# Gates and mask preparation moved later, keys and values moved one slot later over two pairs of banks, and unread products before the scores

## The chip, the cores and the metric

The kernel runs on one core of one Trainium2 chip. The metric is the device time of one execution in microseconds (us), lower is better. Three runs of the kernel before were timed, and one more execution was profiled. The engines are named PE (TensorE), DVE (VectorE), ACT (ScalarE), POOL (GpSimd) and SP (SyncE, which here only issues loads and stores).

## The reference, cut to what matters

One decoder layer in three parts, for 8 sequences of 128 tokens with 256 features:

```python
x = x + gated_delta_attention(layernorm(x))       # 16 heads, DK = 128, VE = 256
x = x + cross_attention(layernorm(x), ctx, mask)  # 16 heads of 8, softmax with a mask
x = x + ffn(layernorm(x))                         # shared expert + top 2 of 8 experts
```

The first part, for every head:

```python
q, k = l2norm(silu(conv4(xn @ Wq))), l2norm(silu(conv4(xn @ Wk)))
v = silu(conv4(xn @ Wv))
alpha, beta = sigmoid(xn @ Wa), sigmoid(xn @ Wb)   # the "gates"
state = state * alpha_t                            # for every t
state = state + beta_t * k_t (v_t - state k_t)
out_t = state q_t ;  result = out @ Wo
```

The second part treats features as rows: queries, keys and values are products of a 128x128 matrix with 128 rows of 256 columns, one per sequence, plus bias; scores are `mask * q.k / sqrt(8) - (1 - mask) * 1e6`, then softmax and the product with the values.

## The kernel before, in words

Every engine has its own program, written out by hand; semaphores (`wait_ge`, `then_inc`) tie them together. So the order of the work is the order in which the functions are called on each engine.

**Start.** SP loads x and the constants, then the weights of the first heads. DVE takes the moments of x (`moments`, L898, L901), ACT turns them into a scale (`norm_act`, L649, L651), DVE normalises (L907), PE turns the result (L1264), ACT copies it out as 32-bit and 16-bit values (L660, L662), DVE takes the low half (L919, `xtl`). PE makes the gate products with Wa and Wb (L1269), DVE copies them (L921), ACT takes Abs, Exp and Ln (L665 to L669), DVE forms `gl` (L928), PE sums over time (L1272), DVE copies and subtracts (`gcum` L930, `gcol` L933). DVE also prepares the mask rows (`mask5`, L924, L936) and the bias rows (`bias5`, L925, L938, L940) for the second part. POOL issues eight loads for the second part (L445), and then splits the weights of a head into 16-bit high and low halves (`split`, L455 to L461).

**The loop of steps.** 32 steps: 16 heads, each for two groups of 4 sequences. `slots` calls `slot(k)` for k = -3 to 33 on every engine, and one slot holds different stages of neighbouring steps: `a` (step k+2) is projected (`proj_`, L1294: 6 products of 512 columns for each of 4 tiles), biased by ACT (L697) and convolved by DVE (`tap`, L1004, 3 for each tile); its squares are split (POOL `sql`, L477). `b0` (step k+1) has its norms (L1322, L1323), logs (ACT L723), exponents (L1339, L1344) and Gram products (L1354, L1364), and DVE multiplies these with the decay (`lm`, L1016, L1027). `b` (step k) inverts a triangular matrix by levels: POOL cuts out the levels (`ct`, L491), PE multiplies (L1374, L1382, L1389, L1392), ACT copies (L679, L684), DVE subtracts (L958 to L987). `z` (L1310) multiplies values with Wo. `c` (step k-1) does the last levels, a residual (L1440 to L1442) and `y` (L1452, L1453, L1463), and `d` (step k-2) the output products (`outp`, L1474), which DVE adds to x (L1034, L1041). Slot 30 has no projection any more, slot 31 no exponents, slot 32 and 33 only `c` and `d`.

Projections and z use the banks `ubank` (PSUM banks 0 and 1), exponents and Gram products `ebank` (2 and 3).

**Keys and values of the second part.** In slots 30 and 31 (`STEPS - 2`, `STEPS - 1`), `kv(n)` handles one sequence bb = 0 to 7 for n = 0 to 3: first the value product of the sequence before (`v_proj`, L1480), then four key products (L1503, each with its bias, L1504) into `ubank`; ACT copies both halves (`k_split`, L768), DVE stacks them (`kv_stack`, `kst`, L1078) and adds the value bias (`v_add`, L1065). POOL masks the context for this at the end of slot 29 (L548).

```python
if m == 1:
    need(pe, v_ready, 2 * bb)
for g2 in range(2):
    o = ubank[hh][:, g2 * H:(g2 + 1) * H]
```

**Scores.** After the loop 64 units follow, four for each of 16 heads. For each unit PE makes `top_scores` (L1584: 4 products of 32 rows) into one of three pairs of banks, DVE reduces it to maxima (`maxima`, L1138); nine units later PE makes `energies` (L1605, 4 products of 32 rows), ACT takes the exponentials (L817), and PE multiplies with the values (`values`, L1619). `pair_free` waits until the pair of banks has been read. Per head there are also query products (`q_proj`, L1571, L1572), their copy (ACT L811) and stacking (DVE L1131), and the turning of the maxima (L1594). Then the feed-forward part follows, which the change doesn't touch.

Of the kernel before, what the change touches and what calls it, by code (L numbers as in the profile page):

```python
# [17 lines left out]
ALU = mybir.AluOpType  # L18
# [103 lines left out]
def build(nc, d, out):  # L122
    with ExitStack() as whole:
# [86 lines left out]
        zrow = zz[0:5].rearrange("p r j n -> p (r j n)")  # L210
# [73 lines left out]
        names = ("x_loaded", "consts_loaded", "xattn_loaded", "experts_loaded", "ffn_loaded", "stored")  # L284
        x_loaded, consts_loaded, xattn_loaded, experts_loaded, ffn_loaded, stored = [sem(n) for n in names]
# [37 lines left out]
        ebank = [bank[2], bank[3]]  # L323
        bt, bx, ctk, cx = [quad[:, n, :] for n in range(4)]
# [35 lines left out]
        def _(sp):  # L360
            for b in range(B):
                sp.dma_start(x1[:, b, :], x_in[:, b, :]).then_inc(x_loaded, 16)
# [63 lines left out]
        def _(pool):  # L426
# [15 lines left out]
            for dst, src in ((maskrow[:], d["mask_row"].partition_broadcast(P)),  # L442
                             (wks[:], d["xk"]), (wvt[:], d["xv"]), (stackcol[:], d["stackcol"]), (biasf, d["xbias"]),
                             (bvrow[:], d["bv_row"].partition_broadcast(P)), (maskcol[:], d["mask_col"]), (wqs[:], d["xq"])):
                g.dma_start(dst, src).then_inc(xattn_loaded, 16)  # L445

# [17 lines left out]
            pool.wait_ge(xn_done, B)  # L464
            split(0, 0, None)
            def slot(k):
# [187 lines left out]
        def _(act):  # L654
            s = nc.scalar
            norm_act(act, 0, slice(0, B))

            for b in range(B):
                act.wait_ge(xt_psum, b + 1)
                s.activation(xt[:, :, b * T:(b + 1) * T], bank[b % 2][:, 0:H].rearrange("p (c t) -> p c t", c=CH), ACT.Copy).then_inc(xt_full, 1)  # L660
# [3 lines left out]
            act.wait_ge(gate_step, 1)  # L664
            s.activation(ga[:], gz[:], ACT.Abs).then_inc(gate_act, 1)  # L665
            act.wait_ge(gate_act, 1)
            s.activation(ga[:], ga[:], ACT.Exp, scale=-1.0).then_inc(gate_act, 1)
            act.wait_ge(gate_act, 2)
            s.activation(ga[:], ga[:], ACT.Ln, bias=1.0).then_inc(gate_act, 1)  # L669

            def slot(k):
                f, a, b0, b, c, d = [k.at(n) for n in (3, 2, 1, 0, -1, -2)]

# [87 lines left out]
                def k_split(n):  # L761

                    if k.i is None and k.c in (STEPS - 2, STEPS - 1):
                        bb = (k.c - STEPS + 2) * 4 + n
                        for m in range(2):
                            act.wait_ge(k_psum, 2 * bb + m + 1)
                            need(act, k_stack, 2 * bb + m - 1)
                            s.activation(kh[:, 1 - m], ubank[1 - m], ACT.Copy).then_inc(k_high, 1)  # L768
# [19 lines left out]
                bias(1)  # L788
                k_split(1)
# [120 lines left out]
        def _(dve):  # L910
# [5 lines left out]
            for b in range(B):  # L916
# [3 lines left out]
            dve.wait_ge(gate_psum, 1)  # L920
            v.tensor_copy(gz[:], bank[2][:, 0:B * 2 * HK]).then_inc(gate_step, 1)  # L921
            dve.wait_ge(xattn_loaded, 16 * 8)
            dve.wait_ge(mask_cast, 1)
            v.tensor_copy(mask5[0:4], maskrow[0:4]).then_inc(mask_cast, 1)  # L924
            v.tensor_copy(biash, biasf).then_inc(bias_cast, 1)  # L925
            dve.wait_ge(gate_act, 3)
            dve.wait_ge(gate_step, 1)
            v.scalar_tensor_tensor(out=gl[:].rearrange("p b n -> p (b n)"), in0=gz[:], scalar=0.0, in1=ga[:], op0=ALU.min, op1=ALU.subtract).then_inc(gate_step, 1)  # L928
            dve.wait_ge(cum_psum, 1)
            v.tensor_copy(gcum[:].rearrange("p h b -> p b h"), bank[3][:, 0:B * HK].rearrange("p (b h) -> p b h", b=B)).then_inc(gates_done, 1)  # L930
            dve.wait_ge(gates_done, 1)
            dve.wait_ge(gate_step, 2)
            v.tensor_tensor(gcol[:].rearrange("p h b -> p b h"), gl[:, :, HK:], gcum[:].rearrange("p h b -> p b h"), ALU.subtract).then_inc(gates_done, 1)  # L933
            dve.wait_ge(mask_cast, 2)
            m5 = mask5[0:4].rearrange("p b n -> p (b n)")
            v.scalar_tensor_tensor(out=m5, in0=m5, scalar=stackcol[0:4, 3:4], in1=maskrow[0:4].rearrange("p b n -> p (b n)"), op0=ALU.mult, op1=ALU.add).then_inc(mask_ready, 1)  # L936
            dve.wait_ge(bias_cast, 1)
            v.tensor_copy(bias5[:], biash).then_inc(bias_cast, 1)  # L938
            dve.wait_ge(bias_cast, 2)
            v.scalar_tensor_tensor(out=bias5[0:4].rearrange("p k g n -> p (k g n)"), in0=biash[0:4].rearrange("p k g n -> p (k g n)"),  # L940
                                   scalar=stackcol[0:4, 2:3], in1=biasf[0:4].rearrange("p k g n -> p (k g n)"), op0=ALU.mult, op1=ALU.add).then_inc(bias_ready, 1)

            def slot(k):
# [877 lines left out]
```

## Time and profile before

| | |
|---|---|
| Timed runs | 937.96 (median), 933.4, 1081.68 us |
| Profiled execution, its own time | 934.79 us |
| Span, first to last instruction | 932.9 us |
| PE busy | 828.1 us (89%) |
| DVE busy | 719.7 us (77%) |
| ACT busy | 617.8 us (66%) |
| POOL busy | 540.2 us (58%) |
| Mean granted clock of PE | 0.94 |

The granted clock is a share of 2.4 GHz; PE has two levels, 1.2 GHz (0.5) and 2.4 GHz (1.0). Times in rows count from the first instruction. In rows of the timeline and of the chain the first number is the start, the second the duration in us; "x12" says how many instructions a row merges.

### The profile page before, as it was taken

To read this page: it belongs to the slowest core of one execution; us is meant where nothing else is said; L and a number is where in the kernel's file an instruction comes from. 1 tells how busy PE (TensorE), PEld (TensorE's weight loads), DVE (VectorE), ACT (ScalarE), POOL (GpSimd) and SP (SyncE) were. 2 spreads that over 40 slices of the span, in tenths; PEclk is the share of its full clock that TensorE was granted. 3 is DMA by queue.
4 is the path that set the end of the run, shared out by engine and by line. 5 is a ranking of instruction groups with operands and counts; after the bars stand their busy time and mean duration, and the time that the engine had idled before them with its cause. 6 is when DMAs were issued, how large, how long until landed. Compare 5 with 4: busy or idle time off the path is not lost.

```text
span 932.9 us, 21903 instructions
## 1 busy us (share of the span) xinstructions
PE 828.1 (89%) x7371; PEld 531.5 (57%) x7408; DVE 719.7 (77%) x1227; ACT 617.8 (66%) x1022; POOL 540.2 (58%) x689
## 2 busy tenths in 40 slices
PE   3578999999999999999999999998867898889997
PEld 2245776677667766777677767765543333323353
DVE  7768888888888888887888788884556756674746
ACT  3377887788778877887888778873230565567522
POOL 6439769678696796886966968574302232322300
PEclk9989999999999999999999999999985777778999
DMA  6202010010110100101101000000001500000000
GB/s 194 57 1 80 1 35 27 11 35 0 34 34 0 34 19 15 34 0 34 34 0 34 10 23 11 2 2 1 1 1 27 94 15 18 16 14 25 10 23 24
DMA packets 34416, 23.98 MB, mean 26 GB/s; under 512 B 5062, under 2 KB 33414, under 8 KB 34235
## 3 DMA queue, kind: packets, MB, share of 16 engines
q1 hardware_dynamic: 31643, 19.00, 7.2%
q0 software_dynamic: 2720, 4.29, 2.2%
q8 instruction: 32, 0.52, 0.2%
q14 instruction: 21, 0.17, 0.1%
HBM read 22.68 MB, written 1.05 MB: 25 GB/s over the span
## 4 chain that ended last, share of the span: by engine, by line
PE 66%; DVE 17%; issue 9%; ACT 5%; POOL 2%; DVEq 1%; DMA 0%; SPq 0%; ACTq 0%; POOLq 0%
PE psum L1294 13%; PE psum L1310 11%; PE psum L1474 6%; DVE y L1004 6%; PE psum L1619 3%; PE psum L1571 3%; PE psum L1364 3%; PE psum L1354 3%; DVE mx L1138 3%; DVE ux L984 3%; PE psum L1382 2%; PE psum L1503 2%; PE psum L1389 1%; PE psum L1392 1%; PE psum L1708 1%
## 5 line engine op out<-in xcount | busy, mean ns | idle before, releaser
L1004 DVE SCALAR_TENSOR_TENSOR y<-psum,cwh,y 128x508 f32<-128x508 f32 (+2 forms) x384 | 281.5, 740 | 18.4 <-ACT y L697 12.4
L491 POOL TENSOR_TENSOR ct<-lm,levels 128x256 f16<-128x256 f32 x224 | 152.0, 701 | 18.4 <-DVE lm L1027 18.4
L477 POOL TENSOR_TENSOR sql<-sq,sqh 128x1024 f16<-128x1024 f32 x32 | 68.4, 2137 | 126.3 <-ACT sq L744 126.3
L697 ACT ACTIVATE y<-psum,cwh 128x512 f32<-128x512 f32 x128 | 99.4, 777 | 50.8 <-PE psum L1294 50.8
L1310 PE MATMUL psum<-wo,vt 128*128 128x256 f32 x512 | 126.0, 389 | 1.2 <-DVE y L1004 1.0
L1310 PEld LDWEIGHTS psum<-wo,vt 128*128 128x128 f32 x512 | 92.3, 190 | 11.9 <-DVE y L1004 2.0
L817 ACT ACTIVATE et<-psum 128x1024 f32<-128x1024 f32 x64 | 65.2, 1022 | 43.3 <-PE psum L1605 43.3
L1138 DVE TENSOR_REDUCE mx<-psum 128x4 f32<-128x1024 f32 x64 | 77.2, 1219 | 21.4 <-PE psum L1584 21.3
L1294 PE MATMUL psum<-xth,whi 128*128 128x512 f16 x256 | 78.0, 387 | 8.7 <-DVE y L1004 5.4
L984 DVE TENSOR_TENSOR ux<-ux,psum 128x512 f16<-128x512 f16 x64 | 43.9, 686 | 53.8 <-PE psum L1392 52.7
L1294 PE MATMUL psum<-xth,wlo 128*128 128x512 f16 x256 | 78.0, 387 | 0.0
L1294 PE MATMUL psum<-xtl,whi 128*128 128x512 f16 x256 | 77.9, 387 | 0.0
L509 POOL TENSOR_TENSOR lml<-lm,lmh 128x1024 f16<-128x1024 f32 x32 | 68.3, 2135 | 0.0
L972 DVE TENSOR_TENSOR ux<-ux,psum 128x512 f16<-128x512 f16 x96 | 65.1, 678 | 1.1 <-PE psum L1392 0.8
L1389 PEld LDWEIGHTS psum<-t1z,ux 128*128 128x128 f16 x768 | 46.9, 98 | 32.4 <-ACT t1z L679 2.5
L1382 PE MATMUL psum<-ux,ct 128*128 128x64 f16 x768 | 54.7, 194 | 11.3 <-DVE ux L984 7.3
L1474 PE MATMUL psum<-zz,pt 128*128 128x256 f32 x256 | 62.4, 388 | 0.7 <-ACT pt L717 0.7
L499 POOL TENSOR_TENSOR lmh<-lm,zero 128x1024 f16<-128x1024 f32 x32 | 60.5, 1891 | 0.0
L1389 PE MATMUL psum<-t1z,ux 128*128 128x64 f16 x768 | 54.3, 194 | 3.4 <-ACT t1z L684 1.9
L595 POOL TENSOR_SCALAR mxs<-mx 128x16 f32<-128x16 f32 x16 | 4.0, 253 | 88.2 <-DVE mx L1138 88.2
L1474 PEld LDWEIGHTS psum<-zz,pt 128*128 128x128 f32 x256 | 49.5, 194 | 7.9 <-ACT pt L717 1.0
L1382 PEld LDWEIGHTS psum<-ux,ct 128*128 128x128 f16 x768 | 36.7, 97 | 30.0 <-DVE ux L984 12.7
(215 smaller groups left out, 2016.6 us busy)
## 6 DMA issues: line engine op xcount, KB each, us to landing
wraw<-in_L_attn_Wv SPq DMA_DIRECT2D x32, 128.0 KB, 2.7
wo<-in_L_attn_Wo SPq DMA_DIRECT2D x16, 256.0 KB, 2.8
wraw<-in_L_attn_Wk SPq DMA_DIRECT2D x16, 128.0 KB, 2.5
wraw<-in_L_attn_Wq SPq DMA_DIRECT2D x16, 128.0 KB, 2.7
moved<-avs SPq DMA_DIRECT2D x128, 16.0 KB, 1.8
x<-in_x SPq DMA_DIRECT2D x8, 128.0 KB, 4.1
maskrow<-in_mask_row POOLq DMA_DIRECT2D x1, 1024.0 KB, 4.5
xt<-in_ctx SPq DMA_DIRECT2D x1, 1024.0 KB, 6.1
```

Source lines behind the costliest of these rows:

```text
L477: g.tensor_tensor(lo, f, hi, ALU.subtract).then_inc(sq_split, 1)
L491: g.tensor_tensor(dst, src, pick.unsqueeze(1).to_broadcast([P, NB, T // (2 * m), m]), ALU.mult).then_inc(masked[l], 1)
L509: g.tensor_tensor(lo, f, hi, ALU.subtract).then_inc(lm_low, 1)
L697: s.activation(y[:, n], ubank[n % 2].rearrange("p (j t) -> p j t", j=NB), ACT.Identity, scale=cwh[:, (a.c // 2) % 2, n, TAPS - 1:TAPS], bi ...
L984: v.tensor_tensor(changed(r, m), changed(r, m), cx.rearrange("p (a q u) -> p a q u", a=2, u=m), ALU.subtract).then_inc(uxc_sb, 1)
L1004: v.scalar_tensor_tensor(out=y[:, n, :, sh:], in0=u[:, :, 0:T - sh], scalar=cwh[:, (a.c // 2) % 2, n, TAPS - 1 - sh:TAPS - sh], in1=y[:, n ...
L1138: v.tensor_reduce(mx[:, h % 2, g2, 2 * rp:2 * rp + 2].rearrange("p r a -> p (r a)"), pair_of("max", n).rearrange("p r (a s) -> p (r a) s", ...
L1294: mm = t.matmul(ubank[n % 2], w_[:, hr, n, ch, :], x_[:, ch, cols], start=(m == 0), stop=(m == len(ops) - 1))
L1310: mm = t.matmul(ubank[n][:, j * H:(j + 1) * H], vt[:, r, vc, (2 * n + j) * T:(2 * n + j + 1) * T], wo[:, hr, vc, :], start=(vc == 0), stop ...
L1382: mm = t.matmul(half(dst[:, j * 64:(j + 1) * 64], m), ct[:, st.c % 2, level, j], first_half(turned(st.c % 2, 1, j), m), start=True, stop=True)
L1389: mm = t.matmul(half(dst[:, 256 + j * 64:256 + (j + 1) * 64], m), turned(st.c % 2, 0, j), first_half(t1z[:, level - 1, j * T:(j + 1) * T], ...
L1474: mm = t.matmul((ctk, cx)[hf][:, jj * H:(jj + 1) * H], pt[:, j], zz[:, d.c % 2, j], start=True, stop=True)
```

## The change

1. Start: a semaphore for each x load, so that the moments of a sequence wait only for its own load. ACT loads at once the table set that holds both Exp and Ln. The turned x goes through other banks (4 and 5). POOL's eight loads for the second part stand behind the first split, which no longer waits for the normalised x. PE's first projections wait for 4 and then 8 low halves only.
2. Gates: products, activations and sums move from ahead of the loop into slot -2, between its projections and taps. The bias rows are prepared at the end of slot -1 (`prepare_bias`), the mask rows at the end of slot 0 (`prepare_mask`), both on DVE.
3. Keys and values: slots 31 and 32 instead of 30 and 31; sequences alternate between `ubank` and `ebank` (`kbank`), and a sequence's key products stand ahead of the value product of the one before.
4. Scores: `warm` puts products of 128 rows and 256 columns, 16-bit, that nobody reads, into the pair of banks ahead of the real ones: 3 before the maxima of the first 8 units, 4 before the exponents of the first 8, 1 before the exponents of the others.

```diff
-            for dst, src in ((maskrow[:], d["mask_row"].partition_broadcast(P)),
...
-                g.dma_start(dst, src).then_inc(xattn_loaded, 16)
...
             pool.wait_ge(conv_scaled, 3)
-            pool.wait_ge(xn_done, B)
             split(0, 0, None)
+            for dst, src in ((maskrow[:], d["mask_row"].partition_broadcast(P)),
...
         def _(act):
             s = nc.scalar
+            s.preload_act_table_set("natural_log_exp_and_others")
             norm_act(act, 0, slice(0, B))
...
-                    dve.wait_ge(x_loaded, 16 * B)
+                    dve.wait_ge(x_loaded[b], 16)
...
+                def prepare_bias():
+
+                    if k.i is None and k.c == -1:
+                        dve.wait_ge(xattn_loaded, 16 * 8)
+                        v.tensor_copy(biash, biasf).then_inc(bias_cast, 1)
...
+                def prepare_mask():
+
+                    if k.i is None and k.c == 0:
+                        dve.wait_ge(xattn_loaded, 16 * 8)
...
                 def kv_stack(n):
 
-                    if not (k.i is None and k.c in (STEPS - 2, STEPS - 1)):
-                        return
-                    bb = (k.c - STEPS + 2) * 4 + n
-                    if n > 0:
-                        v_add(bb - 1)
+                    if not (k.i is None and k.c in (STEPS - 1, STEPS)):
+                        return
+                    bb = (k.c - STEPS + 1) * 4 + n
...
                     pe.wait_ge(w_split, a.head + 1)
+                    if k.i is None and k.c in (-2, -1):
+                        pe.wait_ge(xt_low, (k.c + 3) * NB)
...
+                def gate_products():
+
+                    if k.i is None and k.c == -2:
+                        for b in range(B):
+                            pe.wait_ge(xt_full, b + 1)
...
                     for m in range(2):
                         hh = 1 - m
+                        need(pe, k_stack, 2 * (bb - 1))
                         if m == 1:
-                            need(pe, v_ready, 2 * bb)
+                            need(pe, v_ready, 2 * (bb - 1))
                         for g2 in range(2):
-                            o = ubank[hh][:, g2 * H:(g2 + 1) * H]
+                            o = kbank[bb % 2][hh][:, g2 * H:(g2 + 1) * H]
...
+                    if n > 0:
+                        v_proj(bb - 1)
...
+            def warm(out, b, gq, count):
+
+                for w in range(count):
+                    t.matmul(out[:, w % 2, 0:H], ident16[:], kst[:, b, gq, :], start=True, stop=True)
+
             def top_scores(n):
...
                 pair_free("max", n)
+                warm(pair_of("max", n), b, gq, 3 if n < 8 else 0)
...
                 pair_free("exp", n)
+                warm(pair_of("exp", n), b, gq, 4 if n < 8 else 1)
```

DVE's order before the first tap and in slot -2. Names are tiles, out<-in; L numbers are lines of the program shown. Before:

```order
L919 TENSOR_TENSOR xtl<-xt,xth 128x2x128 [waits xt_high] x8
L921 COPY gz<-psum 128x256 [waits gate_psum]
L924 CAST mask5<-maskrow 4x2048 [waits mask_cast,xattn_loaded]
L925 CAST zz<-zz 5x1024
L928 SCALAR_TENSOR_TENSOR gl<-gz,ga 128x256 [waits gate_step,gate_act]
L930 COPY gcum<-psum 128x8x16 [waits cum_psum]
L933 TENSOR_TENSOR gcol<-gl,gcum 128x8x16 [waits gate_step,gates_done]
L936 SCALAR_TENSOR_TENSOR mask5<-mask5,stackcol,maskrow 4x2048 [waits mask_cast]
L938 COPY bias5<-zz 5x1024 [waits bias_cast]
L940 SCALAR_TENSOR_TENSOR bias5<-zz,stackcol 4x1024 [waits bias_cast]
L1004 SCALAR_TENSOR_TENSOR y<-psum,cwh,y 128x4x127 [waits biased0]
```

And after the change, from the low halves on, with the end of slot -1 as its last rows (L1025 is `tap`, L1048 `lmul_later`, which was L1027):

```order
L924 TENSOR_TENSOR xtl<-xt,xth 128x2x128 [waits xt_high] x8
L1025 SCALAR_TENSOR_TENSOR y<-psum,cwh,y 128x4x127 [waits biased0]
...
L932 COPY gz<-psum 128x256 [waits gate_psum]
L1025 SCALAR_TENSOR_TENSOR y<-psum,cwh,y 128x4x127 [waits biased2]
...
L939 SCALAR_TENSOR_TENSOR gl<-gz,ga 128x256 [waits gate_step,gate_act]
L941 COPY gcum<-psum 128x8x16 [waits cum_psum]
L944 TENSOR_TENSOR gcol<-gl,gcum 128x8x16 [waits gate_step,gates_done]
...
L950 CAST vv<-vv 5x1024 [waits xattn_loaded]
L952 COPY bias5<-vv 5x1024 [waits bias_cast]
L954 SCALAR_TENSOR_TENSOR bias5<-vv,stackcol 4x1024 [waits bias_cast]
L1048 TENSOR_TENSOR lm<-psum,decay 128x512 [waits decayed,kq_psum]
```

The taps moved ahead of the gates, and the bias rows now stand directly ahead of `lm`; the mask rows stand in the same way ahead of the `lm` of slot 1.

PE's order at a sequence of keys and values in the middle of slot 31. Before, the value product comes first and the second half of the keys waits for `v_ready`:

```order
L1480 MATMUL psum<-wvt,xt 128x128 [waits k_stack]
L1480 MATMUL psum<-wvt,xt 128x128
L1503 MATMUL psum<-xt,wks 128x256 [waits ctx_masked]
L1504 MATMUL psum<-mask5,bias5 128x256
L1503 MATMUL psum<-xt,wks 128x256
L1504 MATMUL psum<-mask5,bias5 128x256
L1503 MATMUL psum<-xt,wks 128x256 [waits v_ready]
L1504 MATMUL psum<-mask5,bias5 128x256
L1503 MATMUL psum<-xt,wks 128x256
L1504 MATMUL psum<-mask5,bias5 128x256
```

After (L1537 and L1538 are the key products, L1513 is `v_proj`):

```order
L1537 MATMUL psum<-xt,wks 128x256 [waits ctx_masked,lm_done]
L1538 MATMUL psum<-mask5,bias5 128x256
L1537 MATMUL psum<-xt,wks 128x256
L1538 MATMUL psum<-mask5,bias5 128x256
L1537 MATMUL psum<-xt,wks 128x256
L1538 MATMUL psum<-mask5,bias5 128x256
L1537 MATMUL psum<-xt,wks 128x256
L1538 MATMUL psum<-mask5,bias5 128x256
L1513 MATMUL psum<-wvt,xt 128x128 [waits k_stack]
L1513 MATMUL psum<-wvt,xt 128x128
```

The value product moved behind the keys of the next sequence, and these no longer wait for `v_ready` here.

PE's order at the first unit of scores, after the change (L1617 is `warm`, L1628 `top_scores`, which was L1584; L1609 and L1610 are the query products):

```order
L1609 MATMUL psum<-xm,wqs 128x256
L1610 MATMUL psum<-mask5,bias5 128x256
L1617 MATMUL psum<-kst,ident16 128x256 [waits q_stack]
L1617 MATMUL psum<-kst,ident16 128x256 x2
L1628 MATMUL psum<-kst,qst 128x256 x4
```

Before, the four products of the unit follow the query products directly. The wait moved from them to the first unread product.

## Rows read from the trace of the kernel before

**Rows 1.** The page, part 4: the chain that ended last, by engine.

```profile
PE 66%; DVE 17%; issue 9%; ACT 5%; POOL 2%; DVEq 1%; DMA 0%; SPq 0%; ACTq 0%; POOLq 0%
```

**Rows 2.** Timeline of the start, 12 to 38 us.

```profile
12.35 1.28 ACT L651 ACT_TABLE_LOAD   x1
12.68 0.60 POOL L445 DMA_DIRECT2D maskrow<-in_mask_row  x1
...
17.43 1.91 POOL L455 TENSOR_TENSOR wraw<-wraw,c 128x1024 f32<-128x1024 f32 x1
...
19.73 6.88 PE L1269 MATMUL psum<-wab,xt 128*128 128x32 f32 x32
...
22.01 2.31 POOL L461 TENSOR_TENSOR wlo<-wraw,whi 128x1024 f16<-128x1024 f32 x1
...
27.10 0.42 ACT L665 ACTIVATE ga<-gz 128x256 f32<-128x256 f32 x1 [6.08 <-DVE gz L921]
...
32.74 2.33 DVE L936 SCALAR_TENSOR_TENSOR mask<-mask,stackcol,maskrow 4x2048 f16<-4x2048 f16 x1
32.83 2.31 POOL L459 COPY cwh<-cb 128x4 f32<-128x4 f32 x1
...
32.93 1.01 PE L1294 MATMUL psum<-xth,whi 128*128 128x512 f16 x2 [1.25 <-issue]
...
35.45 3.03 DVE L940 SCALAR_TENSOR_TENSOR bias<-zz,stackcol 4x1024 f16<-4x1024 f16 x1
```

**Rows 3.** The chain in order of time, slots -2 and -1.

```profile
42.33 0.61 ACT y L697
...
48.11 2.13 POOL sql L477
...
50.94 5.11 PE psum L1294 x12
```

**Rows 4.** Timeline at the ends of slots -1 and 0.

```profile
64.93 0.68 DVE L1027 TENSOR_TENSOR lm<-psum,decay 128x512 f32<-128x512 f32 x1
...
66.74 2.75 POOL L491 TENSOR_TENSOR ct<-lm,levels 128x256 f16<-128x256 f32 x4
...
84.81 2.76 POOL L491 TENSOR_TENSOR ct<-lm,levels 128x256 f16<-128x256 f32 x4
```

**Rows 5.** Chain, slots 30 to 33; the last two rows: timeline, ordinary slot.

```profile
637.66 0.96 PE psum L1480 x4
...
674.03 0.71 PE psum L1480 x4
...
677.95 0.61 ACT kh L768
...
679.38 0.71 PE psum L1480 x4
...
698.48 3.79 PE psum L1474 x8
...
703.94 1.19 PE psum L1571 x2
...
614.12 0.39 PE L1344 MATMUL psum<-rows,select 128*128 128x128 bf16 x4
...
622.92 1.97 PE L1310 MATMUL psum<-wo,vt 128*128 128x256 f32 x8
```

**Rows 6.** Windows: length, busy us per engine (instructions), PEclk, DMA share, GB/s; last, line L1584.

```profile
657.80:687.00 29.20, 25.20 (x182) 16.08 (x179) 15.83 (x28) 8.90 (x18) 8.75 (x9) 1.00 0.01 1
...
712.80:724.40 11.60, 8.57 (x46) 3.50 (x48) 11.33 (x12) 0.60 (x1) 2.19 (x7) 0.50 0.01 1
724.40:841.50 117.10, 102.63 (x965) 36.04 (x961) 79.38 (x94) 67.88 (x85) 31.53 (x90) 0.76 0.17 32
...
762.00:769.70 7.70, 6.33 (x74) 2.48 (x74) 5.77 (x8) 5.05 (x7) 2.15 (x8) 1.00 0.03 8
...
L1584 PEld LDWEIGHTS psum<-kst,qst x256: 90/94/147, 711.1 to 841.9; 32*128 32x128 f16 x128
```

More of the change, by code:

```diff
@@ L927, in _ @@
[L927 to L941, printed above, removed]
@@ L943, in slot, with gate_raw, gate_sums @@
             def slot(k):
                 f, a, b0, b, c, d = [k.at(n) for n in (3, 2, 1, 0, -1, -2)]
+                def gate_raw():
+                    if k.i is None and k.c == -2:
+                        dve.wait_ge(gate_psum, 1)
+                        v.tensor_copy(gz[:], bank[2][:, 0:B * 2 * HK]).then_inc(gate_step, 1)
+                def gate_sums():
+                    if k.i is None and k.c == -2:
+                        dve.wait_ge(gate_act, 3)
+                        dve.wait_ge(gate_step, 1)
+                        v.scalar_tensor_tensor(out=gl[:].rearrange("p b n -> p (b n)"), in0=gz[:], scalar=0.0, in1=ga[:], op0=ALU.min, op1=ALU.subtract).then_inc(gate_step, 1)
+                        dve.wait_ge(cum_psum, 1)
+                        v.tensor_copy(gcum[:].rearrange("p h b -> p b h"), bank[3][:, 0:B * HK].rearrange("p (b h) -> p b h", b=B)).then_inc(gates_done, 1)
+                        dve.wait_ge(gates_done, 1)
+                        dve.wait_ge(gate_step, 2)
+                        v.tensor_tensor(gcol[:].rearrange("p h b -> p b h"), gl[:, :, HK:], gcum[:].rearrange("p h b -> p b h"), ALU.subtract).then_inc(gates_done, 1)
@@ new lines, in prepare_mask @@
+                def prepare_mask():
+                    if k.i is None and k.c == 0:
+                        dve.wait_ge(xattn_loaded, 16 * 8)
+                        dve.wait_ge(mask_cast, 1)
+                        v.tensor_copy(mask5[0:4], maskrow[0:4]).then_inc(mask_cast, 1)
+                        dve.wait_ge(mask_cast, 2)
+                        m5 = mask5[0:4].rearrange("p b n -> p (b n)")
+                        v.scalar_tensor_tensor(out=m5, in0=m5, scalar=stackcol[0:4, 3:4], in1=maskrow[0:4].rearrange("p b n -> p (b n)"), op0=ALU.mult, op1=ALU.add).then_inc(mask_ready, 1)
@@ L1263, in _ @@
                 for c in range(CH):
[L1264 removed]
+                    mm = t.transpose(quad[:, b % 2, c * P:(c + 1) * P], xn[:, b, c * P:(c + 1) * P], ident[:])
                 mm.then_inc(xt_psum, 1)
[L1266 to L1274 removed]
             def slot(k):
@@ L1295, in proj_, with gate_totals @@
                     mm.then_inc(proj[n], 1)
+                def gate_products():
+                    if k.i is None and k.c == -2:
+                        for b in range(B):
+                            pe.wait_ge(xt_full, b + 1)
+                            for c in range(CH):
+                                mm = t.matmul(bank[2][:, b * 2 * HK:(b + 1) * 2 * HK], xt[:, c, b * T:(b + 1) * T], wab[:, c, :], start=(c == 0), stop=(c == CH - 1))
+                        mm.then_inc(gate_psum, 1)
+                def gate_totals():
+                    if k.i is None and k.c == -2:
+                        pe.wait_ge(gate_step, 2)
+                        t.matmul(bank[3][:, 0:B * HK], tri[:], gl[:, :, 0:HK], start=True, stop=True).then_inc(cum_psum, 1)
                 def z(n):
@@ L1317, in norms @@
                     pe.wait_ge(sq_split, b0.count(1, 1))
+                    if k.i is None and k.c == -1:
+                        pe.wait_ge(gates_done, 2)
                     need(pe, lm_done, b0.count(2, 0))
@@ L1479, in v_proj @@
                     for st in range(2):
-                        mm = t.matmul(ubank[0][:, st * P:(st + 1) * P], ctxs[:, bb, st * P:(st + 1) * P], wvt[:], start=True, stop=True)
+                        mm = t.matmul(kbank[bb % 2][0][:, st * P:(st + 1) * P], ctxs[:, bb, st * P:(st + 1) * P], wvt[:], start=True, stop=True)
                     mm.then_inc(v_psum, 1)
                 def kv(n):
-                    if not (k.i is None and k.c in (STEPS - 2, STEPS - 1)):
+                    if not (k.i is None and k.c in (STEPS - 1, STEPS)):
                         return
-                    bb = (k.c - STEPS + 2) * 4 + n
+                    bb = (k.c - STEPS + 1) * 4 + n
                     if bb == 0:
```

89 lines of the change are left out of this document (44 added, 45 removed).

## The prediction

> **What bounds the kernel now.** I read the page's chain first [rows 1]: it runs over TensorE (PE) for 66% of the span and over VectorE (DVE) for 17%, so PE's order and clock decide, and another engine only where PE waits for it. Then, stage by stage, the places that the diff touches.
>
> At the start [rows 2] the first projection stands at 32.93 us. Ahead of it: POOL (GpSimd) issues eight loads from 12.68, splits the first weights from 17.43 to 24.32 (22.01 + 2.31), PE makes the gate products until 26.61, and ACT and DVE turn them into sums. The chain goes on over the third bias at 42.33, the square's low half on POOL at 48.11, and 12 projection products at 5.11 us, which is 427 ns for 512 columns, the 1.2 GHz level [rows 3].
>
> At the loop's end [rows 5] a batch's keys and values repeat every 5.35 us (674.03 to 679.38): 3.92 us of products, then ACT's copy, DVE's stacking and again PE, over one pair of banks. The last output products take 3.79 us at 698.48, half speed.
>
> In the scores [rows 6] the granted clock is 0.76 on average over 117 us, while PE is busy for 102.6 of them. A head (four units) takes 7.7 us where the clock is 1.00; the mean head of the 13 in this stretch takes 9.0. Before that, from 712.8 to 724.4, DVE is busy for 11.33 of 11.6 us: there PE's clock costs nothing.
>
> **The change part by part**, against the profiled execution's own 934.8 us (1.9 around its span of 932.9; the median shown is 3.2 higher, the lowest run 1.4 lower).
>
> *Start, first half.* POOL no longer issues eight loads or waits for x before the first split, so the split can start a little behind 12.68, say 12.9, if the raw weights are there, and ends 6.89 later at 19.8. Statistics per batch and a table load fewer (1.28) bring x forward too; they are hidden, since the projection now waits for the split. First projection: 20.1, 12.8 earlier. Its twelve products at 1.2 GHz take 5.11, the gate products 6.88 behind them, DVE's copy and ACT's three steps (0.42 each, no load between, as both functions are in one set now) about 1.85: 33.9 [rows 2, 3]. There the third bias can run, which ran at 42.33; 0.1 for hand-over, and I take 34.1: -8.2. The taps of the first two tiles lie under the gate products. The gate sums stand between tap 3 of tile 2 and tile 3 (about 2 us, and the last tile's taps then end near 42, beside the low half of the squares, which ends at 42.2 instead of 50.2). Shift here: -8.0. Bounds: -9.5 if the gate products run at the full clock, -6 if weights land 2 us late.
>
> *Start, given back.* The casts and stackings that stood in the shadow of the gates now stand on DVE ahead of the product lm of L1027, at the end of slots -1 and 0; behind lm wait POOL's ct, then PE's first level and all that follows. The bias part in slot -1: POOL's sql starts just ahead of it and ends with the start of ct at 66.74; behind it come two copies (estimate 0.8, a third of the mask's 2.33), the stacking (half of 2.33, 1.2; the rest of its 3.03 at 35.45 was a wait), then lm 0.6: ct 2.6 later [rows 2, 4]. In slot 0 the mask's stacking 2.33 and its cast, taken as half of that, make 3.5; lm and with it ct (84.81) is late by this, less what slack there is, plus a POOL pass caught between: 3.4. Together +6.0. Bounds: +2.6 if nothing collides and most of it passes beside POOL's sql, +8 if POOL is caught twice. Net start -2.0 (-6 to +1).
>
> What a collision does is in rows 2: POOL's copy of 128x4 at 32.83 lasts 2.31 us, as long as DVE's stacking at 32.74; the stacking at 35.45 lasts 3.03 for half the elements of the one that took 2.33. The Trainium skill (SBUF — State Buffer, "Who interferes with whom") says that DVE, with two SBUF inputs or in a two-port mode, and GpSimd take a shared port pair for a whole instruction and the second blocks fully. By that rule the +6.0 stands and +2.6 would be out of reach, as POOL's wlo and sql passes stand there; the trace agrees with it.
>
> *Keys and values a slot later.* Slot 30 loses its four batches. Until 637.66 nothing changes (POOL masks the context there). From there to the start of z at 657.8 [rows 6] it took 20.1; what is left is what an ordinary slot has from its exponents at 614.12 to z at 622.92, 8.8 us, less two projections, each half of what six products take in rows 3, 1.3 [rows 3, 5]: 6.2; I take 6.7, as one more copy stands in series there. Gain 13.4. Slot 31 keeps four batches, now over two pairs: three stalls of 5.35 - 3.92 go, 4.3, but 2.6 of other products stood in them: -1.7. Slot 32 (687.0 to 698.48, 11.5, waits for the most part) takes four batches of 3.92, 15.7, and a last wait of 1.4; 5.5 of it fills that slot's waits: +11.6. The output products then run behind a busy PE at 2.4 GHz: -1.9. Sum -5.4 (-3 to -8).
>
> *Entry to the scores.* The eight query products from 703.94 (1.19 for two) with copy and stacking between them would take 5.4 instead of 8.1 at full clock. I take -2.0 (0 to -2.7), as PE waits twice for 1.5 us there.
>
> *Unread products.* 24 stand before the first 8 maxima, 32 before the first 8 exponents, 56 before the others; a 256-column product takes half of what 512 columns take [rows 3], 0.21 at 1.2 GHz and 0.107 at 2.4. The first 24 lie under DVE's maxima: 8.57 + 24 x 0.21 = 13.7 at half clock would be 2.1 over the 11.6, at full clock there is room: 0. Then 13 heads. With p the share at 1.2 GHz, a head takes 7.65 + 2.8 p: 0.76 is p = 0.48 and gives 9.0, as measured. Four products add 0.43 at full clock and 0.85 at half, of which DVE's work covers some: 0.3 and 0.6 net. What p becomes, no row says. In the slot of 657.8 to 687.0 PE is busy for 86% with whole-array products and has 1.00; in the scores 88% with 32-row products gives 0.76. So whole-array products keep the clock where strips don't, and I take p = 0.2, a bit nearer to the loop: 13 x (7.65 + 0.56 + 0.35) = 111.3 instead of 117.1, -5.8, and +2.0 for the extra 24 of the first exponents: -3.8. Bounds: p = 0, -11.6; p as before, +8.
>
> Each group of four 32-row products loads its weights in 94 ns [rows 6], now beside products in flight. If a whole-array product ahead of the group uncovers that load, the 72 groups with one pay 72 x 0.094 = 6.8 us on PE; I leave it out of the sum and make it a rival.
>
> The Trainium skill (TensorE: Matmul & The Clock Gate, "Part 3: Packing small matmuls") states such a rule: a weight load overlaps products in flight only where their row groups differ, and a whole-array product shares all of them. No row quoted here shows whether it holds at this place.
>
> Sum: -2.0 - 5.4 - 2.0 - 3.8 = -13.2, 921.6; I say **922**.
>
> **The rivals.**
> *Clock held at 2.4 GHz through all scores.* For it: fast stretches of whole heads exist already (762.0 to 769.7). Against it: one product per unit is little. Scores -11.6, entry -2.7, start and loop end -7.4: 913.
> *The clock falls and rises as before.* The products then cost +8, the entry gives nothing: 934.8 - 7.4 + 8 = 935.
> *Slower.* The unread products stand between the bank's release and the real product, and at 1.2 GHz each is twice as dear; if the clock is at 1.2 for more of the scores than now, PE is the bound and they are all on its path. Place: the scores after the first maxima. Price at p = 0.6: 13 x (7.65 + 1.68 + 0.65) = 129.7, +12.6, and 5.5 for the first groups: 934.8 - 7.4 + 18 = 945. It decides from p of about 0.46 on. Against it: whole-array products are what the loop has, with 1.00.
> *Loads uncovered.* As worked out above, 6.8 us more on PE in the scores, 922 + 6.8 = 929. For it: the strips' loads have cover now and a whole-array product takes all rows. Against it: PE isn't on the path all the time in a head at full clock (6.33 of 7.7 busy).
> *The start isn't shorter.* If weights or DVE and POOL collisions eat all 8 us and the loop's end gives 3: 934.8 - 3 - 2 - 3.8 = 926.
>
> **How the numbers follow.** Forecast 0.38, clock held 0.25, as before 0.14, loads uncovered 0.10, start not shorter 0.07, slower 0.06. A measurement of this kernel can tell about 2% from no change: under 919.2 is faster, over 956.7 slower (against 937.96). Faster: 0.85 of the clock-held case and a quarter of the forecast, 0.31. Slower: a third of its case, 0.02. The range reaches from under the clock-held case to just over the as-before one: 911 to 936. It leaves out the slower case and some of the ends.
>
> **What would show it.** First projection near 20 us; POOL's first sql near 40; ct of slot 0 about 5.5 and of slot 1 about 2 us earlier than 66.7 and 84.8; z of the last step near 642; last output products at full clock, ending near 695; first maximum near 703.6. In the scores: mean granted clock of 0.9 and heads of 8.4 to 8.6 us. Wrong if the clock there stays under 0.8, if heads at full clock take over 8.1 us (the products cost more than counted), or if the first lm (L1027 before) doesn't come near 60.

## The result

| | median, us | runs | ratio to before, 95% interval |
|---|---|---|---|
| before | 936.2 | 933.4, 934.47, 937.96, 1081.68 | |
| changed | 993.7 | 990.57, 990.74, 996.69, 996.89 | 1.0619, 1.0571 to 1.0667 |

The changed kernel is 6.2% slower; I had said 922 us, 911 to 936. Its profiled execution took 990.57 us with a span of 988.8, against 934.79 and 932.9: 55.9 us more. The run of 1081.68 us is a slow one and isn't in the ratio.

The page of the changed kernel: PE's busy tenths and its clock in 40 slices (24.7 us each), the chain by engine (it answers to [rows 1]; the chain could only be followed back to 612.8 us, so its shares cover 38% of the span), and two groups of instructions with their busy time, mean ns and the idle time ahead of them.

```profile
PE   3678999999999999999999999798899999999897
...
PEclk9798999999999999999999999896755555557999
...
PE 32%; DVE 2%; issue 2%; ACT 1%; POOL 1%; DVEq 0%; POOLq 0%; ACTq 0%
...
L822 ACT ACTIVATE et<-psum 128x1024 f32<-128x1024 f32 x64 | 65.5, 1023 | 88.4 <-PE psum L1650 87.9
L1164 DVE TENSOR_REDUCE mx<-psum 128x4 f32<-128x1024 f32 x64 | 78.2, 1223 | 52.1 <-PE psum L1628 50.2
```

The same two groups on the page of before:

```profile
L817 ACT ACTIVATE et<-psum 128x1024 f32<-128x1024 f32 x64 | 65.2, 1022 | 43.3 <-PE psum L1605 43.3
L1138 DVE TENSOR_REDUCE mx<-psum 128x4 f32<-128x1024 f32 x64 | 77.2, 1219 | 21.4 <-PE psum L1584 21.3
```

The reader sees the loss in one look: seven slices in a row with PE at 9 and the clock at 5, and ACT and DVE, whose own work hasn't grown, waiting 45 and 31 us longer for PE's scores. Stretch by stretch (windows of the changed kernel, columns as in [rows 6]):

```profile
641.10:701.90 60.80, 52.79 (x318) 32.07 (x314) 32.46 (x67) 18.15 (x34) 9.56 (x11) 0.86 0.00 1
672.50:689.50 17.00, 15.74 (x65) 8.59 (x64) 5.60 (x14) 4.83 (x9) 0.00 (x0) 0.50 0.00 1
709.80:727.70 17.90, 17.63 (x83) 6.54 (x84) 13.17 (x14) 1.24 (x3) 2.18 (x7) 0.50 0.00 1
727.70:896.00 168.30, 168.30 (x1038) 50.80 (x1036) 81.97 (x92) 69.93 (x84) 31.57 (x90) 0.50 0.12 23
```

The fourth row answers to the third of [rows 6]: 168.3 us instead of 117.1, PE busy for all of it, the clock at 0.50 throughout instead of 0.76. The third answers to its second: the first maxima took 17.9 us instead of 11.6, and now PE is busy for 17.63 of them and DVE waits. The account: 2.0 us were gained up to the first query product (701.95 against 703.94), and 57.9 lost behind it (988.8 - 701.9 = 286.9 against 932.9 - 703.9 = 229.0).

Why a head costs so much stands in a timeline of one of its units at 1.2 GHz (L1628: the maxima's strips, 4 products of 32 rows; L1617: the unread product; L1650: the exponents' strips; L1664: values), with the starts of the query products one head apart:

```profile
786.17 1.22 PE L1609 MATMUL psum<-xm,wqs 128*128 128x256 f32 x2
...
794.06 0.61 PE L1628 MATMUL psum<-kst,qst 32*128 32x256 f16 x4
794.60 0.39 PE L1617 MATMUL psum<-kst,ident 128*128 128x256 f16 x1
794.93 0.61 PE L1650 MATMUL psum<-qst,kst 32*128 32x256 f16 x4
795.47 1.08 PE L1664 MATMUL psum<-et,vz 128*32 128x256 f32 x8
...
798.89 1.22 PE L1609 MATMUL psum<-xm,wqs 128*128 128x256 f32 x2
```

and in the kernel before, the last two units of a head in which the clock was at 1.2 GHz too (L1584, L1605, L1619 are the same products):

```profile
747.04 1.22 PE L1571 MATMUL psum<-xm,wqs 128*128 128x256 f32 x2
...
753.53 0.61 PE L1584 MATMUL psum<-kst,qst 32*128 32x256 f16 x4
754.19 0.61 PE L1605 MATMUL psum<-qst,kst 32*128 32x256 f16 x4
754.73 1.08 PE L1619 MATMUL psum<-et,vz 128*32 128x256 f32 x8
755.75 0.39 PE L1584 MATMUL psum<-kst,qst 32*128 32x256 f16 x2
755.76 0.40 PE L1605 MATMUL psum<-qst,kst 32*128 32x256 f16 x2
755.94 0.42 PE L1584 MATMUL psum<-kst,qst 32*128 32x256 f16 x2
755.95 0.42 PE L1605 MATMUL psum<-qst,kst 32*128 32x256 f16 x2
756.30 1.08 PE L1619 MATMUL psum<-et,vz 128*32 128x256 f32 x8
...
757.31 1.22 PE L1571 MATMUL psum<-xm,wqs 128*128 128x256 f32 x2
```

Before, the two sets of strips ran interleaved in the last unit: a strip of each started at the same moment, as one set uses two of the array's row groups and the other set (nine units behind, an odd number) the other two. All eight took 756.30 - 755.75 = 0.55 us. With a product of all rows between them they run one set after the other: 0.54 + 0.33 + 0.54 = 1.41. So the unread product cost 0.86 us where I had counted 0.21: 0.33 of its own, from its start to that of the next strip, and 0.53 of lost company. Not every unit had that much to lose. In the one behind the turning of the maxima (753.53) the exponents' strips wait for DVE's step on the turned maxima (L1126, 753.96), the sets ran one after the other before too, in 1.20 us, and the price was 0.21. The two units behind the query products took 0.74 and 0.75 and now 1.60 and 1.41. Over the four units that is 2.6 us, 0.65 on average. A head went from 10.27 (757.31 - 747.04) to 12.72 (798.89 - 786.17) at the same clock. The Trainium skill (TensorE: Matmul & The Clock Gate, "Part 3: Packing small matmuls") states the other half of the rule that I had cited: products in different row groups run at the same time in one array. The trace of before agrees (755.75 and 755.76), and I had not looked at what stood next to the place of the new product.

Two theories for the rest, and a third for the clock. *Between strips*: the products' place makes PE the bound at 1.2 GHz, and from there the clock doesn't come back. *Own time*: any further product would do it. *Entry*: the moved keys and values send PE into the scores with a low clock, and it stays there.

### The profile page after: what moved, and what is told of

It reads as the page before. It is cut to its first block and busy times, and to the rows that moved or that the text cites. A ratio compares the mean times of both kernels' runs of the same rounds, so it can differ in the third digit from the quotient of the medians.

```text
span 988.8 us, 22137 instructions
## 1 busy us (share of the span) xinstructions
PE 904.0 (91%) x7483; PEld 549.1 (56%) x7520; DVE 725.2 (73%) x1227; ACT 617.4 (62%) x1020; POOL 537.4 (54%) x689
## 5 line engine op out<-in xcount | busy, mean ns | idle before, releaser
L1025 DVE SCALAR_TENSOR_TENSOR y<-psum,cwh,y 128x508 f32<-128x508 f32 (+2 forms) x384 | 281.5, 740 | 21.7 <-ACT y L701 15.7
L1664 PE MATMUL psum<-et,vz 128*32 128x256 f32 x512 | 64.5, 596 | 0.0
```

Source lines behind the costliest of these rows:

```text
L1025: v.scalar_tensor_tensor(out=y[:, n, :, sh:], in0=u[:, :, 0:T - sh], scalar=cwh[:, (a.c // 2) % 2, n, TAPS - 1 - sh:TAPS - sh], in1=y[:, n ...
L1664: mm = t.matmul(avb[ps, gq // 2 * H:(gq // 2 + 1) * H], vz[:, b % 2, st, r, gq], et[:, gn % 4, r, st], start=(gq == 0 and st == 0), stop=( ...
```

## The experiments

All changes below are against the changed kernel unless "before" is said. The kernel before ran beside each set: 935.2, 933.7 and 933.5 us.

### Without the unread products, and each group of them alone

```diff
-                warm(pair_of("max", n), b, gq, 3 if n < 8 else 0)
+                warm(pair_of("max", n), b, gq, 0)
-                warm(pair_of("exp", n), b, gq, 4 if n < 8 else 1)
+                warm(pair_of("exp", n), b, gq, 0)
```

> The changed kernel without any unread product. Between strips: a whole-array product between the 32-row strips of two units ends their running side by side and costs about 0.6 us a unit at 1.2 GHz; without it heads go back to 9.0 us on average, the granted clock in the scores to about 0.76, and the time to 928 to 936 us (the scores began 3 us earlier than in the kernel before). Entry: the moved keys and values leave PE at 1.2 GHz and it stays there without the products too; the heads then take the 10.3 us that the slow heads of the kernel before took, and the time is about 960.

Measured: 931.5 us, ratio 0.995 (0.9921 to 0.9978). Windows of the first maxima, and from there to the last maximum:

```profile
714.70:727.10 12.40, 9.19 (x48) 3.64 (x48) 11.38 (x12) 1.13 (x3) 2.19 (x7) 0.50 0.01 2
727.10:841.20 114.10, 99.53 (x960) 35.28 (x960) 79.93 (x93) 67.47 (x85) 31.54 (x90) 0.79 0.17 33
```

The whole loss is gone, with the clock at 0.79 (0.76 in the kernel before). The entry theory fell here: with all the moves in place the stage doesn't stay low by itself.

The two groups apart: the first eight units only (3 and 4 products, none for the others), or the others only (0, and 1 at each exponent).

> The changed kernel with the unread products at the first eight maxima (3 each) and exponents (4 each) alone. Between strips: those 56 cost 6 to 12 us at most (exponents 4 x 0.21 to 0.33 us x 8 at 1.2 GHz), then heads go as in the kernel before: 932 to 944. Entry, or a clock that stays low once PE is filled: 965 or more, clock 0.5 through the scores.

Measured: 943.6 us, ratio 1.0097 (1.0063 to 1.013), 12 us over the run without any. The 56 products of the first groups don't hold the clock down afterwards, but they bring nothing back: they cost 0.21 us each, and in the profiled execution (948.33) the first rise of the clock comes at 748 instead of 735.

> The changed kernel with one unread product ahead of each exponent's strips from the ninth unit on, and none at the first eight. Between strips: close to the changed kernel, 975 to 992, clock 0.5 to 0.55 over the heads. Own time alone: 56 x 0.21 = 12 us over the run without any, 940 to 948, clock 0.7 or more.

Measured: 927.9, 942.77, 943.46 and 970.76 us. No ratio can be given; the clock took different courses in the four executions (its mean over the span was 0.952, 0.932, 0.932 and 0.891). Of the profiled one (943.46), two windows that follow each other:

```profile
739.00:810.70 71.70, 64.82 (x678) 24.41 (x674) 50.19 (x53) 45.03 (x55) 20.32 (x56) 1.00 0.14 27
810.70:855.10 44.40, 44.40 (x289) 13.36 (x290) 22.47 (x33) 20.60 (x26) 8.82 (x27) 0.50 0.05 13
```

My expected 975 to 992 was a miss: the product between the strips doesn't force the low clock. While the clock is at 1.00 it stays there for 71.7 us. But once it fell, at 810.7, after 2.70 us in which PE was busy for 1.94, it stayed down for 44.4 us with PE busy for all of them. In the kernel before, between the first rise at 735 and the last maximum, these are the longest stretches at either level:

```profile
745.50:759.10 13.60, 13.47 (x97) 4.30 (x97) 6.87 (x7) 6.93 (x9) 3.37 (x12) 0.50 0.08 21
786.40:806.80 20.40, 16.61 (x199) 6.36 (x191) 15.62 (x17) 13.24 (x17) 5.10 (x14) 1.00 0.07 19
```

So the product between the strips lengthens both: the high clock holds, and the low one does too.

### The same products, one place earlier

```diff
-                warm(pair_of("max", n), b, gq, 3 if n < 8 else 0)
+                warm(pair_of("max", n), b, gq, 0 if n < 8 else 1)
-                warm(pair_of("exp", n), b, gq, 4 if n < 8 else 1)
+                warm(pair_of("exp", n), b, gq, 0)
```

> The changed kernel with the same 56 unread products moved ahead of the maxima's strips from the ninth unit on, so that the maxima's and the exponents' strips stay next to each other. Between strips: they cost their own 0.21 to 0.33 us, strips still interleave, clock above 0.6, time 938 to 960, at least 20 us under the run with one per exponent. If any further product on PE does it, both runs take the same time.

Measured: 922.1 us, ratio 0.9863 (0.9805 to 0.9922); once more in the last set:

> The run with one unread product per maximum and all moves (922.1 before), once more for its interval: 920 to 925, ratio 0.985 to 0.99.

921.9 us, ratio 0.9889 (0.9872 to 0.9905): 1.1% under the kernel before, an interval clear of 1 but less than the 2% that I had set as a change, and 7% under the changed one. Windows of the first of the two runs (first maxima; up to the clock's rise; the rest), and its unit at 1.2 GHz, in which the strips of both sets start together again behind the unread product:

```profile
710.00:723.10 13.10, 10.07 (x50) 3.74 (x50) 11.66 (x13) 1.19 (x2) 2.19 (x7) 0.50 0.00 1
723.10:738.10 15.00, 14.32 (x101) 4.66 (x101) 10.06 (x11) 7.67 (x8) 4.72 (x11) 0.50 0.47 84
738.10:840.50 102.40, 92.65 (x1023) 36.68 (x1022) 75.02 (x93) 68.28 (x86) 29.77 (x85) 1.00 0.13 26
```

```profile
731.82 0.39 PE L1617 MATMUL psum<-kst,ident 128*128 128x256 f16 x1
732.15 0.39 PE L1628 MATMUL psum<-kst,qst 32*128 32x256 f16 x2
732.16 0.40 PE L1650 MATMUL psum<-qst,kst 32*128 32x256 f16 x2
732.33 0.42 PE L1628 MATMUL psum<-kst,qst 32*128 32x256 f16 x2
732.35 0.42 PE L1650 MATMUL psum<-qst,kst 32*128 32x256 f16 x2
732.70 1.08 PE L1664 MATMUL psum<-et,vz 128*32 128x256 f32 x8
```

The whole unit, from the unread product to the values, takes 732.70 - 731.82 = 0.88 us, against 1.41 in the changed kernel. And the clock holds at 1.00 for 102.4 us on end. What I had as a rival (the clock held through the scores) exists, with one product per unit, at this place.

The changed kernel with only its single product moved by that one place, the first groups left as they are:

```diff
-                warm(pair_of("max", n), b, gq, 3 if n < 8 else 0)
+                warm(pair_of("max", n), b, gq, 3 if n < 8 else 1)
-                warm(pair_of("exp", n), b, gq, 4 if n < 8 else 1)
+                warm(pair_of("exp", n), b, gq, 4 if n < 8 else 0)
```

> The changed kernel, with the single product from the ninth unit on put ahead of the maxima's strips instead of between them and the exponents' strips; the number of products stays. Between strips: the clock rises at 735 to 755 and holds, 925 to 940. If the products of the first eight groups alone send the stage into the low clock whatever follows: 975 or more.

Measured: 935.2 us, ratio 1.0012 (0.9978 to 1.0045). The number of unread products is the same as in the changed kernel, and it takes 58 us less. Its windows, while the clock was down and up, in an execution of 943.39 us; eight of its ten runs took 933 to 937, with a mean clock of 0.947 to 0.952 against 0.938 in this one, so the rise mostly came sooner than here:

```profile
709.60:764.20 54.60, 54.33 (x285) 18.90 (x283) 28.13 (x31) 12.62 (x15) 9.28 (x28) 0.50 0.29 52
764.20:859.80 95.60, 86.66 (x961) 34.37 (x957) 70.28 (x87) 64.49 (x82) 28.51 (x82) 1.00 0.07 18
```

The clock rises at 764 here, 26 us later than without the first groups (738), and then holds past the last maximum (853). This is the decisive pair: the place, not the number; the own-time theory falls with it. Read with the runs before it: without the first groups the clock mostly found its way up although the products stood between the strips, and with the first groups it found its way up as long as they didn't. The changed kernel has both, and there it stayed down to the end of the scores in the execution that was profiled; the mean clock of its four runs, 0.869 to 0.875, says the same of the others.

Next, the four at the first exponents are taken out too (3 at the first eight maxima, 1 at the others, none at an exponent).

> As the run before, and none at the first eight exponents either: 3 at the first eight maxima, 1 at every other maximum. Between strips: no unread product is left between strips, clock up by 740, 917 to 926, with that of one per maximum alone (922) in its middle; first maxima filled with products should bring the rise forward by 3 to 10 us, or take 2 us on PE. If the filling of the first maxima is what holds the clock down: 935 or more.

Measured: 926.5 us, ratio 0.9924 (0.9893 to 0.9955). So the 32 at the first exponents cost 8.7 us and the 24 at the first maxima 4.5 more (926.5 against 922); with them the clock rose at 741.3 instead of 738.1. I had expected it to come 3 to 10 us sooner: it doesn't.

### The products without the moves

```diff
--- before
+                warm(pair_of("max", n), b, gq, 3 if n < 8 else 0)
+                warm(pair_of("exp", n), b, gq, 4 if n < 8 else 1)
```

> The kernel before with the unread products of the changed kernel (3 at the first eight maxima, 4 at the first eight exponents, 1 at every other exponent) and nothing else of the change. Products alone: the clock stays at 0.5 through the heads, a head 12.7 us, 980 to 1000. If the moved keys and values or the moved gates are needed for it: clock as in the kernel before, 935 to 955.

Measured: 994.1, 996.0 and 996.2 us, and once 963.2. A window of the profiled one:

```profile
691.10:906.10 215.00, 207.76 (x1231) 67.86 (x1231) 106.37 (x135) 80.48 (x102) 42.16 (x115) 0.50 0.10 21
```

The unread products alone make the kernel before as slow as the changed one in three runs of four, and the fourth is still 3.2% over the kernel before. The moved gates, keys and values aren't needed for the loss. The one run at 963.2 has no trace; a clock that rose part of the way through would explain it, and its mean granted clock, 0.925 against 0.877 to 0.881 in the others, fits.

> The kernel before with one unread product ahead of the maxima's strips from the ninth unit on, and nothing else. The moved gates, keys and values brought 3.7 us in the run without products (931.5 against 935.2), so this should be 922 + 3.7 = 926, 922 to 930, with a clock of 1.00 for most of the heads. If the rise of the clock hangs on the moved parts: 932 or more.

(0 for the first eight, then 1 ahead of the maxima's strips, none at the exponents, and no other edit.) Measured: 925.6 us, ratio 0.9925 (0.9881 to 0.9969), the clock at 1.00 from 739.1 on. The gain doesn't hang on the moves either.

### The moves by themselves

The start alone (before, with the gates, loads, bias and mask as in the changed kernel):

> The kernel before with the start of the changed kernel (gates behind the first projection, loads behind the first split, bias and mask prepared in slots -1 and 0) and nothing else. The floors of the last step came 3.2 us earlier in the changed kernel (624.8 against 628.0) and 1.9 in the run without unread products, so 2 to 3 us less than before: 931 to 933. If what is left of my forecast for both moves (9.4 us) came from the start: 926 to 928.

Measured: 934.6 us, ratio 1.0009 (0.9986 to 1.0031). In its trace z of the last step came 2.9 us earlier than before (654.9), but the low clock that begins at the end of the loop lasted 51.2 us (688.8 to 740.0) instead of 44.3 (690.8 to 735.1).

Keys and values alone (before, with `kv`, `v_proj`, `k_split` and `kv_stack` a slot later over both pairs):

> The kernel before with the keys and values a slot later over two pairs of banks and nothing else. My forecast was 5.4 us less, and 2.0 less at the entry of the scores. In the changed kernel the granted clock fell to 0.5 for 17 us over these batches, in the kernel before it stayed at 1.00 there: if that eats the gain, 933 to 937, with the first query product at 703 to 709 against 703.9; if the forecast holds, 926 to 929 and the first query product near 698.

Measured: 934.6 us, ratio 1.0017 (0.9996 to 1.0039). Two stretches of its slots 31 and 32:

```profile
656.20:666.50 10.30, 10.30 (x44) 5.93 (x43) 3.54 (x7) 2.17 (x4) 0.00 (x0) 0.51 0.01 2
680.10:697.20 17.10, 15.84 (x66) 8.47 (x67) 5.97 (x16) 5.50 (x10) 0.00 (x0) 0.51 0.00 1
```

In the kernel before, the granted clock was 1.00 over the batches but for 3.4 us around 638 (slot 31: first row of [rows 6]). Here 27 us of slots 31 and 32 ran at half speed; its first query product came at 710.4, 6.5 us later than before.

> The changed start, keys and values as before, one unread product ahead of the maxima's strips from the ninth unit on. If keys and values a slot later bring nothing: 922 to 924, level with the run that has them. If they are worth what I forecast: 927 or more.

Measured: 924.8 us, ratio 0.9909 (0.9877 to 0.9941), 2.8 us over the run with all moves. The two intervals overlap, so whether keys and values a slot later are worth anything beside a held clock stays open. Both moves together, without an unread product, gave 0.995 (the first run above), each by itself nothing.

## Why the prediction was wrong

**Start: -2.0 forecast.** In the changed kernel the norms of the last step (`n2m` on DVE) came 3.1 us earlier (624.68 against 627.80), so the net was about right, from two larger errors that cancelled. That was luck. From its timeline:

```profile
20.39 1.04 PE L1312 MATMUL psum<-xth,whi 128*128 128x512 f16 x2 [2.54 <-POOL wlo L458]
...
24.72 3.65 PE L1321 MATMUL psum<-wab,xt 128*128 128x32 f32 x32
...
36.05 2.27 POOL L477 TENSOR_TENSOR sql<-sq,sqh 128x1024 f16<-128x1024 f32 x1
...
55.94 1.27 DVE L954 SCALAR_TENSOR_TENSOR bias<-vv,stackcol 4x1024 f16<-4x1024 f16 x1
...
57.89 2.75 POOL L491 TENSOR_TENSOR ct<-lm,levels 128x256 f16<-128x256 f32 x4 [2.98 <-DVE lm L1048]
...
73.77 2.14 POOL L477 TENSOR_TENSOR sql<-sq,sqh 128x1024 f16<-128x1024 f32 x1
73.92 3.06 DVE L962 CAST mask<-maskrow 4x2048 f16<-4x2048 f32 x1
77.02 2.34 DVE L965 SCALAR_TENSOR_TENSOR mask<-mask,stackcol,maskrow 4x2048 f16<-4x2048 f16 x1
...
80.04 2.75 POOL L491 TENSOR_TENSOR ct<-lm,levels 128x256 f16<-128x256 f32 x4 [4.13 <-DVE lm L1048]
```

First projection 20.39, as forecast (20.1). The gate products then took 3.65 us, not 6.88, as the clock was up; I had that as a bound, and the first sql stood at 36.05, 12.0 earlier where I took 8.0. Given back were 8.9 instead of 6.0: ct of slot 0 came 8.8 earlier than its 66.74, that of slot 1 4.8 earlier than its 84.81, from then on 3.1. So the bias part gave back 3.2 (2.6 forecast), the mask part 4.0 (3.4 forecast), and 1.7 went later, for which I had no term. The mask's two steps took 5.40 us against my 3.5, and the cast is the reason. In the kernel before it had taken what I put:

```profile
26.98 1.20 DVE L924 CAST mask<-maskrow 4x2048 f16<-4x2048 f32 x1
```

In its new place it started 0.15 us behind POOL's `sql` and ended 1.07 behind that one's end (73.77 + 2.14 = 75.91, 73.92 + 3.06 = 76.98): it waited for POOL. The cast of the bias rows did the same (0.67 us before, 2.40 now at 53.06, beside the `sql` of 52.78). So the collision that I had read from rows 2 was real, and it makes 1.9 of the 5.40; the stackings, with no POOL instruction beside them, took 2.34 and 1.27. On the end time the start alone brought nothing that could be measured (1.0009).

**Keys and values: -5.4 forecast.** The mechanism was right for slot 30: z of the last step stood at 641.1, 13.6 us sooner beyond the start's 3.1 (forecast 13.4). The step that failed is the next: slots 31 and 32 were priced at full clock, and the output products "behind a busy PE at 2.4 GHz" as a bonus. From z to the first query product it took 60.8 us where my terms give 54.1. The trace has the reason:

```profile
657.65 0.70 PE L1537 MATMUL psum<-xt,wks 128*128 128x256 f32 x2
...
673.94 1.22 PE L1537 MATMUL psum<-xt,wks 128*128 128x256 f32 x2
```

The same two key products take 0.70 us at 2.4 GHz and 1.22 at 1.2, and the clock stood at 0.50 for 17 us from 672.5 on (second window of the result). Just ahead of its fall PE had waited three times for steps of the inversion's last levels on DVE and ACT, busy for 1.96 of 4.00 us:

```profile
668.00:672.00 4.00, 1.96 (x29) 1.37 (x27) 2.92 (x7) 0.61 (x2) 0.00 (x0) 1.00 0.00 0
```

How long it stays down differs between executions of the same instructions. From z to the first query product it took 58.5 us where the clock was down for 10.2 (one per maximum), 60.8 with 17.1 (the changed kernel) and 65.2 with 27.2 (without unread products, 653.1 to 663.3 and 677.0 to 694.0). Drawn on to no low clock, that is 54 to 55, an estimate from these three, and my terms gave 54.1: they were right at full clock, and the clock is what they had wrong. The output products did run at full clock (1.74 us at 698.5 instead of 3.79), but ended at 700.3, not near 695. Alone, the move took as long as it saved (1.0017).

**Entry: -2.0 forecast.** In the run without unread products, the first maximum stood 714.7 - 707.5 = 7.2 us behind the first query product, against 8.9 before: -1.7. Right. In the changed kernel it was 7.9 (709.81 - 701.95).

**Unread products: -3.8 forecast, +58 measured on everything from the first query product on.** Three steps failed:

- *The price*, 0.21 us at 1.2 GHz, 0.85 a head. It was 0.65 a unit on average, 2.45 a head, as the timelines above show. The rival "loads uncovered" had the right place (the product of all rows beside strips) and a part of the sum, 0.33 - 0.21 = 0.12 us (the 94 ns of its row are the load of one product, not of four); the larger part, the two sets of strips running together, I hadn't seen. It was in the timeline of before. At full clock the price was smaller: a head took 7.58 us in the kernel before (792.57 to 800.15), 8.33 with the product between the strips (one per exponent, 762.69 to 771.02) and 7.92 with it ahead of them (one per maximum, 761.79 to 769.71). So +0.3 at 2.4 GHz, as forecast, holds for the other place only; at the place of the change it was 0.75, and the head is over my sign of 8.1.
- *The clock*, p = 0.2. It was 1. "Whole-array products keep the clock where strips don't" was half right: one such product a unit did hold the clock at 1.00 for 102 us where it stood ahead of the strips. But the argument spoke only of holding it, and the stage begins at 0.50, so what had to be forecast was the rise.
- *The first groups*, 0 under the maxima and 2.0 at the exponents. PE was at work for 17.63 us in the first maxima, not 13.7; without them they took 12.4. Together the first groups cost 12 to 13 us.

Of the 51 us more between the first exponent and the last maximum (727.7 to 897.6 against 725.1 to 843.8), 13 heads times 12.72 - 10.27 make 32, and the clock's share, 13 times 10.27 - 9.0, makes 17; 2 us are left.

Among the rivals *Slower* had place and mechanism: PE the bound, the products on its path, the clock at 1.2 GHz for more of the scores. Its size was off: it was priced at p = 0.6 and got 0.06. My own formula at p = 1 gives 7.65 + 2.8 = 10.45 a head without them (10.27 in the trace), + 0.85; that alone would have said 934.8 - 7.4 + 13 x (11.3 - 9.0) + 5.5 = 963. The range ended at "as before", p = 0.48, though no row said what p would become, and my own bounds for it should have run from 0 to 1.

**The clock.** In row after row it stood at 0.50 with PE busy for the whole of the stretch: 168.3 of 168.3 us, 44.4 of 44.4, 54.33 of 54.6. The Trainium skill (TensorE: Matmul & The Clock Gate, "Part 1: The HAM clock gate") says that activity releases the throttle. These rows don't bear that out if activity means a busy PE as the profile counts it; the measurement decides. What the chip goes by in its place isn't shown here. Shown is only that the same products in another order let it rise.

## What to carry to other kernels

Before a whole-array product is put in a stream of small ones, look in the timeline at what starts together there: the price is its own time plus the overlap that it breaks, and it is dearer at the low clock (here 2.45 us a head against 0.75). A filler against a low clock belongs ahead of two packed groups that run together, not between them. The 56 in the first eight units, where the clock stood at 0.50, cost 12 us and brought nothing. When an instruction is moved to another engine's busy stretch, look at what stands there on the engine that it can collide with: two casts, 0.67 and 1.20 us long, became 2.40 and 3.06. And when a stage has two courses, forecast both ends, p = 0 and p = 1, and let the range reach them.

## What was not expected of the hardware

- The low clock can last as long as the work does: 168 us at 0.50 with PE busy throughout, and 44 us in a run that had held 1.00 for 72 us just before, with the same instructions.
- One product of 256 columns in each unit was enough to hold 1.00 for 102 us, in a stage where the clock before changed between its levels every 3 to 20 us.
- The course isn't fixed by the program: one kernel (one product per exponent) took 927.9 to 970.8 us on one chip in four runs, with a mean granted clock of 0.952 to 0.891. In other kernels the same instructions ahead of the scores ran with the clock down for 10, 17 or 27 us.
- A DVE cast of 4 rows of 2048 elements from 32 to 16 bit took 1.20 us by itself and 3.06 when it started just behind a POOL instruction of 2.14 us. The stacking of the same rows took 2.34.
